# Moving the shared expert's products and sums of a first FFN from VectorE to ScalarE and GpSimd, and splitting the inversion of the routing marks into quarters

## What is computed

```
x = x + 0.5 * ffn(layernorm(x))
x = x + attention(layernorm(x))
x = x + 0.5 * ffn(layernorm(x))        # the same ffn weights

ffn(x): scores = softmax(x @ gate_w.T); choose 2 of 16 experts per token
        y = sum over the two of weight * ((silu(x @ We1 + be1) * (x @ We3 + be3)) @ We2 + be2)
        z = (silu(x @ ws1 + bs1) * (x @ ws3 + bs3)) @ ws2 + bs2      # the shared expert, for every token
        return y + z
```

## Time and profile before

| what | value |
| --- | --- |
| time of the program, median of 3 runs | 1203.08 us (1202.75 to 1204.58) |
| the profiled execution | span 1200.4 us; its own time outside the profile is not given, and the runs lie 2.4 to 4.2 us above the span |
| busy in the span | TensorE 87%, ScalarE 74%, VectorE 65%, GpSimd 36% |
| the front of the first FFN | 0 to about 115 us |
| its loop over the experts' tiles | about 115 to 242 us |

### The profile page before, as it was taken

How to read it: one execution, slowest core, us unless ns; L and a number is a source line. 1 busy time by engine, 2 the same in 40 slices (tenths; PEclk the granted TensorE clock), 3 DMA queues, 4 the chain that set the end, 5 groups by cost and what they waited for, 6 DMA issues and landing times.

```text
span 1200.4 us, 23553 instructions
## 1 busy us (share of the span) xinstructions
PE 1041.7 (87%) x7485; PEld 559.3 (47%) x7486; DVE 782.3 (65%) x1624; ACT 883.2 (74%) x1305; POOL 436.6 (36%) x531
## 2 busy tenths in 40 slices
PE   2997999979886788998889889988897988999995
PEld 2455999945554211222122222222223568998854
DVE  7798777758996414444344456486576788778855
ACT  2326777736887999999999999999995326777710
POOL 1002666557720323221111121420211424777755
PEclk9998999989999899999999999999998999999998
DMA  7910555545766101010202021120100854666654
GB/s 252 282 59 22 168 166 166 154 123 163 228 207 214 53 18 54 18 49 10 63 10 62 10 94 44 32 68 19 45 1 1 279 164 126 184 186 176 177 165 144
DMA packets 125715, 133.77 MB, mean 111 GB/s; under 512 B 13224, under 2 KB 111888, under 8 KB 125616
## 3 DMA queue, kind: packets, MB, share of 16 engines
q1 hardware_dynamic: 109056, 90.95, 23.8%
q0 software_dynamic: 14448, 39.47, 12.1%
q10 hardware_dynamic: 2112, 2.10, 0.5%
HBM read 80.43 MB, written 52.04 MB: 110 GB/s over the span
## 4 chain that ended last, share of the span: by engine, by line
PE 25%; ACT 21%; issue 18%; DVE 10%; POOL 3%; DVEq 1%; DMA 1%; ACTq 0%; POOLq 0%
ACT wide L1961 20%; PE banks L2298 5%; PE banks L2223 4%; PE banks L1845 3%; PE banks L1820 2%; PE banks L2310 2%; PE banks L2232 2%; POOL f_region L1281 2%; PE banks L1859 2%; PE banks L2286 1%; DVE x_res L1535 1%; POOL f_stage L2415 1%; DVE wide L1562 1%; DVE attn_lines_parts L211 1%; PE banks L1373 1%
## 5 line engine op out<-in xcount | busy, mean ns | idle before, releaser
L1961 ACT ACTIVATE wide<-banks 128x1536 f32<-128x1536 f32 (+1 forms) x448 | 506.0, 1278 | 22.9 <-PE banks L1820 22.5
L1845 PE MATMUL banks<-wide,attn_attend_v_now 128*32 128x512 f32 (+3 forms) x2560 | 300.9, 545 | 0.1
L1977 POOL TENSOR_SCALAR_AFFINE_SELECT wide<-wide 128x512 f32<-128x512 f32 (+2 forms) x176 | 89.6, 524 | 453.1 <-ACT wide L1961 452.9
L1820 PE MATMUL banks<-attn_attend_q_now,attn_attend_k_now 32*128 32x512 f16 (+3 forms) x1280 | 159.0, 358 | 67.9 <-ACT wide L1961 63.4
L1820 PEld LDWEIGHTS banks<-attn_attend_q_now,attn_attend_k_now 32*128 32x128 f16 x1280 | 43.2, 91 | 322.1 <-ACT wide L1961 293.9
L624 POOL DMA_INDIRECT f_region<-xn_rows,f_token_of x79 | 79.6, 1008 | 135.1 <-DVE f_token_of L843 93.6
L2298 PE MATMUL banks<-f_xnt 128*128 128x128 f32 x752 | 102.8, 280 | 10.9 <-DVE f_more L2524 9.4
L2014 DVE RECIPROCAL below<-below 128x512 f32<-128x512 f32 x32 | 107.3, 3353 | 1.1
L2298 PEld LDWEIGHTS banks<-f_xnt 128*128 128x128 f32 x752 | 92.3, 193 | 16.8 <-issue 10.5
L2029 DVE TENSOR_TENSOR x_res<-banks,x_res 128x512 f32<-128x512 f32 x30 | 20.7, 690 | 112.9 <-PE banks L1859 112.9
L2009 DVE COPY sums<-banks 128x512 f32<-128x512 f32 x32 | 22.1, 691 | 110.0 <-PE banks L1845 109.1
(11 more groups left out here) (357 smaller groups left out, 1788.9 us busy)
## 6 DMA issues: line engine op xcount, KB each, us to landing
y_half<-f_xnt SPq DMA_DIRECT2D x94, 128.0 KB, 2.3
y_slots<-wide SPq DMA_DIRECT2D x79, 128.0 KB, 1.7
attn_v<-f_more SPq DMA_DIRECT2D x32, 256.0 KB
attn_attend_v_now<-attn_v SPq DMA_DIRECT2D x32, 256.0 KB, 3.0
x_res<-L_attn_x SPq DMA_DIRECT2D x8, 512.0 KB, 7.7
xn_rows<-f_w_all SPq DMA_DIRECT2D x8, 512.0 KB, 2.8
attn_q<-attn_lines_q_out SPq DMA_DIRECT2D x8, 512.0 KB, 3.7
attn_k<-attn_lines_k_out SPq DMA_DIRECT2D x8, 512.0 KB, 3.6
```

Of the source, the lines that this page charges most:

```text
L1820: last = pe.matmul(score[i % SLOTS][:, j, c0:QW], k_now[rows, kt * P:(kt + 1) * P], q_now[rows, qc * QW + c0:(qc + 1) * QW], start=True, s ...
L1845: last = pe.matmul(out_bank[qc][rows, c0:QW], v_now[:, kt, rows], probs[:, place_of[HG * u + h], c0:QW], start=(kt == 0), stop=(u == last_ ...
L1961: act.activation(probs[:, at:at + n, c0:QW], score[i % SLOTS][:, 0:n, c0:QW], ACT.Exp, scale=SCALE).then_inc(sem.exp_done, 1)
L1977: pool.affine_select(out=part, in_=part, compare_op=ALU.is_ge, fill=0.0, base=0, pattern=[[0, end - begin], [1, P]], channel_multiplier=-1 ...
```

## The change

VectorE keeps the routing alone. ScalarE, besides silu, keeps banks 2 and 3 with their bias in `s_lin` (two buffers of 128 x 512 with one use each, lent by the attention), and keeps half of banks 4 and 5 in `s_out`. GpSimd, working from these copies, multiplies `s_lin` by `s_silu` (12 instructions) and adds `s_out` to x (12). Of the four quarters of tile marks GpSimd scales quarters 0 and 2, one instruction each, and ScalarE quarters 1 and 3 as before, one instruction a pair. VectorE marks rows of quarters 0 and 1 before tiles of 2 and 3. TensorE makes the counts ahead of the third block, inverts quarters 0 and 1 ahead of block 5 and quarters 2 and 3 ahead of down 5. GpSimd brings four rows' tiles, then adds the last block's sums, then brings on; VectorE waits for those sums ahead of the loop.

```diff
+    core.s_lin = (core.sums[:], core.below[:])
+    core.s_out = (part(2 * D), core.w_o[:].rearrange("p g d -> p (g d)"))
...
@@ TensorE
             def shared_up(i, products=range(4)):
                 for f in products:
                     if i >= 1:
-                        if f < 2:
-                            pe.wait_ge(sem.silu_ready, 2 * (i - 1) + f + 1)
-                        else:
-                            pe.wait_ge(sem.prod_ready, i)
+                        pe.wait_ge((sem.silu_ready, sem.lin_ready)[f // 2], 2 * (i - 1) + f % 2 + 1)
...
             def shared_down(i):
-                pe.wait_ge(sem.prod_ready, i + 1)
+                pe.wait_ge(sem.multiplied, 2 * i + 2)
...
-                            pe.wait_ge(sem.z_added, 2 * (i - 1) + j // 2 + 1)
+                            pe.wait_ge(sem.z_kept, 2 * (i - 1) + j // 2 + 1)
...
+            def invert(part):
+
+                pe.wait_ge(sem.rows_marked, part + 1)
+                pe.wait_ge((sem.pool_scaled, sem.scaled)[part % 2], part // 2 + 1)
+                for q in range(part * PAIRS // 4, (part + 1) * PAIRS // 4):
+                    last = pe.matmul(bank[7][:, 0:SLOT_TILES], row_hot[:, q, :], tile_hot[:, q, :], start=(q == 0), stop=(q == PAIRS - 1))
+                last.then_inc(sem.inverted, 1)
...
             shared_up(0)
             shared_up(1)
             shared_down(0)
-            shared_up(2)
-            shared_down(1)
             pe.wait_ge(sem.shifted, 2)
             pe.wait_ge(sem.pairs_ready, 1)
             pe.matmul(bank[6][:, :], core.before[:], assigned[:], start=True, stop=True)
             pe.matmul(bank[7][:, :], core.ones[:], assigned[:], start=True, stop=True).then_inc(sem.counted, 1)
-            for i in range(3, EARLY):
+            for i in range(2, EARLY - 1):
                 shared_up(i)
                 shared_down(i - 1)
-            pe.wait_ge(sem.hot_ready, 2)
-            for q in range(PAIRS):
-                last = pe.matmul(bank[7][:, 0:SLOT_TILES], row_hot[:, q, :], tile_hot[:, q, :], start=(q == 0), stop=(q == PAIRS - 1))
-            last.then_inc(sem.inverted, 1)
+            invert(0)
+            invert(1)
+            shared_up(EARLY - 1)
+            shared_down(EARLY - 2)
+            invert(2)
+            invert(3)
             shared_down(EARLY - 1)
...
-                        pe.wait_ge(sem.z_added, 2 * EARLY)
+                        pe.wait_ge(sem.z_kept, 2 * EARLY)
...
@@ ScalarE
             def gate(i, f):
                 act.wait_ge(sem.up_ready, 4 * i + f + 1)
-                if f == 0 and i >= 2:
-                    act.wait_ge(sem.prod_ready, i - 1)
+                if i >= 2:
+                    act.wait_ge(sem.multiplied, 2 * (i - 2) + f + 1)
                 act.activation(s_silu[:, i % 2, f, :], bank[f][:, :], ACT.Silu, bias=bs[:, f:f + 1]).then_inc(sem.silu_ready, 1)
+
+            def keep_lin(i, f):
+                act.wait_ge(sem.up_ready, 4 * i + f + 3)
+                if i >= 1:
+                    act.wait_ge(sem.multiplied, 2 * (i - 1) + f + 1)
+                act.activation(core.s_lin[f], bank[2 + f][:, :], ACT.Identity, bias=bs[:, 2 + f:3 + f]).then_inc(sem.lin_ready, 1)
+
+            def keep_products(i):
+                for f in range(2):
+                    gate(i, f)
+                for f in range(2):
+                    keep_lin(i, f)
+
+            def keep_out(i):
+                for j in range(2):
+                    act.wait_ge(sem.down_ready, 2 * i + j + 1)
+                    if i >= 1:
+                        act.wait_ge(sem.z_added, 2 * (i - 1) + j + 1)
+                    act.activation(core.s_out[j], bank[4 + j][:, :], ACT.Copy, scale=0.5).then_inc(sem.z_kept, 1)
...
-            for i in range(EARLY - 1):
-                gate(i, 0)
-                gate(i, 1)
+            keep_products(0)
+            for i in range(1, EARLY - 2):
+                keep_products(i)
+                keep_out(i - 1)
             act.wait_ge(sem.half_ready, 1)
-            scale_marks(0)
+            keep_products(EARLY - 2)
+            keep_out(EARLY - 3)
             scale_marks(1)
-            gate(EARLY - 1, 0)
-            gate(EARLY - 1, 1)
-            scale_marks(2)
-            scale_marks(3).then_inc(sem.hot_ready, 1)
+            scale_marks(3)
+            keep_products(EARLY - 1)
+            keep_out(EARLY - 2)
             act.wait_ge(sem.stage_stored, 16 * BLOCKS)
             act.activation(w_all[:, :, UP - 2:UP], be_kept[:].rearrange("p a e -> p e a"), ACT.Copy).then_inc(sem.be_ready, 1)
+            keep_out(EARLY - 1)
...
@@ GpSimd
+            def multiply(i):
+                for f in range(2):
+                    pool.wait_ge(sem.silu_ready, 2 * i + f + 1)
+                    pool.wait_ge(sem.lin_ready, 2 * i + f + 1)
+                    if i >= 2:
+                        pool.wait_ge(sem.down_ready, 2 * (i - 1))
+                    pool.tensor_tensor(s_prod[:, i % 2, f, :], core.s_lin[f], s_silu[:, i % 2, f, :], ALU.mult).then_inc(sem.multiplied, 1)
+
+            def add_shared(i):
+                for j in range(2):
+                    pool.wait_ge(sem.z_kept, 2 * i + j + 1)
+                    pair = x[:, i * BT + 2 * j:i * BT + 2 * j + 2, :].rearrange("p n d -> p (n d)")
+                    pool.tensor_tensor(pair, pair, core.s_out[j], ALU.add).then_inc(sem.z_added, 1)
+
+            def scale_marks(part):
+                pool.wait_ge(sem.half_ready, 1)
+                pool.wait_ge(sem.marked, part + 1)
+                some = slice(part * PAIRS // 4, (part + 1) * PAIRS // 4)
+                pool.tensor_tensor(tile_hot[:, some, :], tile_hot[:, some, :], value_of[:, some].rearrange("p (q o) -> p q o", o=1)
+                                   .to_broadcast([P, PAIRS // 4, SLOT_TILES]), ALU.mult).then_inc(sem.pool_scaled, 1)
+
+            multiply(0)
+            multiply(1)
+            add_shared(0)
+            multiply(2)
+            add_shared(1)
+            scale_marks(0)
+            multiply(3)
+            add_shared(2)
+            scale_marks(2)
+            for i in range(4, EARLY):
+                multiply(i)
+                add_shared(i - 1)
             pool.wait_ge(sem.stage_stored, 16 * BLOCKS)
             pool.wait_ge(sem.tokens_ready, 1)
-            for n in range(FIRST_TURNS):
+            for n in range(ROUND):
+                bring(n)
+            add_shared(EARLY - 1)
+            for n in range(ROUND, FIRST_TURNS):
                 bring(n)
...
@@ VectorE: all of multiply and add_shared goes; at the end
             mark_tiles(0)
-            multiply(4)
             mark_tiles(1)
+            mark_rows(0)
+            mark_rows(1)
             mark_tiles(2)
             mark_tiles(3)
-            add_shared(3)
-            mark_rows(0, PAIRS // 2)
-            multiply(5)
-            mark_rows(PAIRS // 2, PAIRS).then_inc(sem.hot_ready, 1)
-            add_shared(4)
+            mark_rows(2)
+            mark_rows(3)
...
-            dve.wait_ge(sem.inverted, 1)
+            dve.wait_ge(sem.inverted, 4)
...
-            add_shared(5)
+            dve.wait_ge(sem.z_added, 2 * EARLY)
```

More of the change, by code:

```diff
@@ L336, in ffn @@
                          "be_ready widened xnt_ready logits_ready logits_kept logits_turned "
-                         "route_step shifted exp_ready pairs_ready counted slots_ready hot_ready marked inverted tokens_ready "
-                         "up_ready silu_ready prod_ready down_ready z_added "
+                         "route_step shifted exp_ready pairs_ready counted slots_ready rows_marked marked pool_scaled scaled inverted tokens_ready "
+                         "up_ready silu_ready lin_ready multiplied down_ready z_kept z_added "
                          "rows_turned rows_kept up_kept down_kept up_done gated_ready prod_done "
@@ L475, in _ @@
             pe.matmul(bank[7][:, :], core.ones[:], assigned[:], start=True, stop=True).then_inc(sem.counted, 1)
[L476 removed]
+            for i in range(2, EARLY - 1):
                 shared_up(i)
                 shared_down(i - 1)
[L479 to L482 removed]
+            invert(0)
[4 more added lines that the diff above has]
+            invert(3)
             shared_down(EARLY - 1)
             pe.wait_ge(sem.silu_ready, 2 * EARLY)
[L486 removed]
+            pe.wait_ge(sem.lin_ready, 2 * EARLY)
             def emit(n, j, r):
@@ L550, in scale_marks @@
                     last = act.activation(tile_hot[:, q, :], tile_hot[:, q, :], ACT.Copy, scale=value_of[:, q:q + 1])
-                return last
+                last.then_inc(sem.scaled, 1)
             take_root(0)
@@ L676, in _ @@
                 normalize(i)
-            def multiply(i):
-                if i >= 2:
-                    dve.wait_ge(sem.down_ready, 2 * (i - 1))
-                for f in range(2):
-                    dve.wait_ge(sem.silu_ready, 2 * i + f + 1)
-                    dve.wait_ge(sem.up_ready, 4 * i + f + 3)
```

(21 more changed lines are left out.)

## The result

The changed kernel takes 1211.5 us (median of 4 runs, 1210.3 to 1213.6) against 1203.2 us: 8.2 us by the medians, and by the ratio of the runs 1.0056, 95% interval 1.0039 to 1.0072, about 7 us slower. Run again later beside the kernel before, it gave 1.0058 (1.0045 to 1.0071).

What follows compares the result with a forecast made beforehand. TensorE bounds the loop (busy 119.7 of 120 us), so the front matters only by when the loop's first turns can run. Inversion 7.6 us later plus loop start 2.6 makes 10.2: 1203.1 to 1213.3 us, range 1204 to 1217.

Steps and rivals of the forecast that it cites:

- the first gap: TensorE ahead of the counts, waiting for `assigned`: idle from 58.0 to 65.4 us, 7.4 us.
- The lock before `assigned`: Six GpSimd instructions ahead of that table hold VectorE up by 4.3 us in all, bounds 0 and 5.8.
- The rival of a weak lock: GpSimd hardly delays VectorE before `assigned`: gap ahead of the counts 3.1 to 4 us, whole 1207; chance 0.20.
- The clock behind it: TensorE after the 7.4 us gap: 4 to 5 us at half clock, 2.1 us lost, bounds 0 and 2.5.
- The second gap: TensorE ahead of the inversion's quarter 1, waiting for ScalarE's scaling behind its copy of down 3: 4.3 us.
- its term for this clock: Half clock on TensorE after the 4.3 us gap within the inversion: 1.3 us lost, bounds 0 and 2.5.
- Not what is late: VectorE's row marks don't delay the inversion: done at 113.8 us at the latest, wanted at 115.
- the bound of 22.5 us: Most that the lock gives back on VectorE up to its marks: 18 x 0.96 + 2 x 2.6 us.
- The rule of the lock: VectorE instructions with two SBUF inputs wait for GpSimd's, those with one don't; 0.96 us per GpSimd product.
- Start of the loop: VectorE enters behind GpSimd's fourth bring and two sums: up 2 comes 2.6 us late, bounds 0 and 3.5.
- Sum: Whole kernel: 7.6 + 2.6 = 10.2 us slower, median from 1203.1 to 1213.3 us.
- The loop can't win it back: TensorE is full in the loop, so the 2.6 us delay of up 2 stays to the end.

Runs made afterwards that it cites:

- e6: e4 with GpSimd's products, sums and scalings cut to 8 columns (scaling one of 80), work left out; inversion done at 61.4 us against 75.6, no comparable ratio.
- e5: Changed kernel, but GpSimd waits for `assigned` between its products of block 0 and block 1; 1.0039 of the kernel before, second chip.
- e3: Changed kernel with VectorE's wait for the last block's sums moved from ahead of the loop to behind its first eight turns; 1.0072 of the kernel before.
- e8: Changed kernel with e3's wait and GpSimd's last two sums behind eight brings instead of four; 1.0110 of the kernel before, second chip.
- r1: Changed kernel run again, unaltered, beside the kernel before; 1.0058 of the kernel before.
- r2: Same kernel as e8, run beside the changed kernel on one chip; 1.0074 of the kernel before.
- e2: Changed kernel with ScalarE scaling quarter 1 ahead of its copies of block 4 and of down 3; 1.0063 of the kernel before.
- e1: Changed kernel with the counts put back behind down 1; 1.0086 of the kernel before.
- e4: Changed kernel with the edits of e1, e2 and e3 together; 1.0074 of the kernel before.
- e7: Kernel before with the inversion in quarters and VectorE's table of experts behind the tokens; 0.9979 of the kernel before, second chip.
- r3: Same kernel as e7, run again on another chip; 0.9963 of the kernel before, 1199.0 us against 1204.7.
- e9: Kernel before with 12 useless 128 x 512 products added on GpSimd, one behind each silu; 1.0017 of the kernel before.

## Why the prediction was right, step by step

**`assigned` and the first gap.** The lock before `assigned` was put at 4.3 us; with GpSimd's work narrowed (e6) it is 24.5 - 20.1 = 4.4. The gap, put at 7.4, was 7.31. Four of the six instructions fell on tables, 0.95 us each for three and 1.07 for one where 0.96 was put, and two fell largely on reductions as laid out (0.23 us each). e5 and e6 show the cause. The rival of a weak lock fell.

**The clock behind it.** The lower level lasted 6.8 us, 3.1 of them behind the restart, where I took 4 to 5. From the counts to block 3's up products TensorE took 76.89 - 64.58 = 12.3 us for 10.8 of work: 1.5 lost, 2.1 predicted. Five executions run alike up to the inversion's end (this one, e3, e8, r1, r2); they lost 1.3 to 2.2.

**The second gap.** 4.21 against 4.3, behind down 3 and ended by ScalarE's sixteenth scaling; e2 shows that ScalarE's order makes it. At the full clock a quarter takes 0.58 us (two in 114.79 to 115.94) and not 0.7, so 102.48 to 115.94 is 13.5 us for 12.0 of work: the clock took 1.4, 1.3 predicted. Inversion: 6.9 us later, 7.6 predicted.

Here the profiled execution was a lucky one. Behind the same gap of 4.2 us the lower level lasted 3.5 us in it, but 6.5 in r1, the same kernel (a stretch, then TensorE's timeline):

```profile
101.10:107.60 6.50, 5.75 (x22) 3.19 (x23) 6.50 (x24) 5.32 (x20) 3.18 (x3) 0.50 0.00 0
```

```profile
102.88 9.60 PE L446 MATMUL banks<-wide 128*128 128x512 f32 x16
```

By the same count r1, e3 and e5 lost 3.0 to 3.1 us to it, more than my bound of 2.5, and e8 and r2 lost 1.6 and 1.7. In the five executions that run alike the inversion ended 76.2 to 77.7 us behind the first shared product, 6.9 to 8.4 later than before's 69.3. The 7.6 fits their middle, but its term for this clock was a guess between bounds that turned out too narrow; what decides between 1.4 and 3.0 stays open.

**VectorE's marks.** "Not what is late" held for the changed kernel itself: 69.2 against the 74.9 at which TensorE asked for the last quarters. But the margin was thin, and I had not drawn the conclusion: VectorE ended 4.4 us later than before although 14.3 us of its work and waits had gone. So GpSimd's work cost VectorE 18.7 us (69.2 against 64.8 - 14.3 = 50.5), within the 22.5 that I had put at most, though a scaling took 3.44 us where I had 2.9. That, not the gaps alone, decides what the split is worth. e1, e2 and e4 take the gaps away, and the time doesn't move, since GpSimd's products and sums then come earlier and meet the marks (15.7 to 15.9 us a half), and TensorE waits for these.

**The rule of the lock.** The prediction said that a VectorE instruction with a single input doesn't wait. That was read too widely from one reciprocal. It did no harm to the number, since the bound of 22.5 us counted every GpSimd instruction, whatever it met. Row marks and copies have a single SBUF tensor input, and waited: a mark of 0.16 us between two GpSimd instructions cost 1.2 us, and the copy in r2 3.36. The Trainium skill (SBUF — State Buffer, the section Who interferes with whom) says that copies, casts and `tensor_scalar` can run in a mode that takes both port pairs and then contend with GpSimd, and that on trn2 reductions never do. The trace agrees for copies, row marks and reductions. Instructions that read banks didn't wait in any row here either.

**Start of the loop.** Inversion to turn 2: 76.2 to 88.1, 11.95 us, against 9.2: 2.75 late, 2.6 predicted. My lower bound, 0 if the sums slipped elsewhere, did not come true in any place tried: e3 brings turn 2 in time and pays at turn 3, e8 and r2 pay in the loop.

**Sum.** Turn 2 was 9.7 us later than before, 10.2 predicted, and 11.1 in r1. The measured whole is 7 to 8 us slower, so 2 to 3 us of the 10.2 are missing. The rows don't show where. "The loop can't win it back" is neither borne out nor refuted: from turn 2 to the last up the changed kernel took 120.0 us against 120.9 before, but 122.6 in r1, with two turns at the lower clock. From the last up to the end of the span it is 960.3 us before, 963.6 after and 959.7 in r1. Single executions differ by more than what is missing. The size of each step up to turn 2 is shown by rows; that the missing part is such scatter is only argued, and that the sum came within 2 us of the median, 1211.5 for 1213.3, is in part luck.

## What to carry to other kernels

Work that is moved from VectorE to GpSimd is only off VectorE if VectorE meanwhile runs what doesn't wait for GpSimd, here reductions and instructions that read banks. Beside tables and marks a sum of 0.64 us on VectorE became 1.27 on GpSimd and about 1 us of waiting on VectorE. When a change opens gaps on the bounding engine, closing them needn't win anything: look which engine would be late next. Narrowing the suspect's work shows in one run what it holds up. Most of the gap that the kernel before had could be filled with nothing moved between engines, by splitting its inversion and putting VectorE's table of experts behind the tokens (e7, r3); neither of these two was run alone.

## What was not expected of the hardware

- Row marks of 0.16 us alternate with GpSimd's instructions one to one: in the changed kernel the first five of 32 took 7.1 us of the 11.6, while GpSimd ran 3.44 + 4 x 1.26 us, and the other 27 came at 0.16 each. A GpSimd product of 1.26 us so costs the marks 1.06 us, about as much as it costs a table (0.95), though a mark alone is a quarter as long as a table.
- A VectorE copy didn't get in between two GpSimd sums that followed each other at once (3.36 us in r2, 2.90 in e8), while marks did.
- A GpSimd product of 128 x 512 whose two inputs are one and the same buffer of 256 columns, read twice over (e9), took 1.04 us; with two different inputs of 512 columns it took 1.26.
- The same idle gap of 4.2 us on TensorE went with 3.5 us at the lower clock in one execution and with 6.5 in another of the same kernel.
